# A gated attention and mixture-of-experts block on one core: short steps moved between engines, one-hot copies and the order list rearranged

## The reference, cut to what matters

```python
x = x + tanh(g_xattn) * cross_attention(layernorm(x), ctx)          # one head of 128, 512 keys
x = x + tanh(g_ffn) * ffn(layernorm(x))

def ffn(X):
    h = rmsnorm(X, norm1_w)
    q, k, v = (h @ w for w in (wq, wk, wv))                          # 16 heads of 8
    ctx = softmax(q @ k.T / sqrt(8)) @ v
    X = X + ctx @ wo
    h2 = rmsnorm(X, norm2_w)
    combine = softmax of the 2 best of 8 experts by softmax(h2 @ router_w)
    return X + swiglu(h2, shared) + sum_e combine[:, e] * swiglu(h2, expert e)
```

## Time and profile before

| | us |
|---|---|
| median of 3 executions (lowest, highest) | 221.26 (218.88, 221.61) |
| the profiled execution | 220.48 |
| its span, from the first to the last instruction | 218.6 |
| TensorE, VectorE, ScalarE, GpSimd busy | 193.9, 139.4, 106.8, 54.6 |

### The profile page before, as it was taken

One profiled execution on the slowest core, in us unless ns is written; L12 is line 12 of the kernel. 1 busy time (PEld: TensorE's weight loads), 2 busy tenths in 40 slices (PEclk: granted clock), 3 DMA queues, 4 the chain that ended last, 5 costly groups with the idle time before them and its releaser, 6 DMA issues.

```text
span 218.6 us, 4395 instructions
## 1 busy us (share of the span) xinstructions
PE 193.9 (89%) x1575; PEld 167.1 (76%) x1575; DVE 139.4 (64%) x357; ACT 106.8 (49%) x215; POOL 54.6 (25%) x88
## 2 busy tenths in 40 slices
PE   7388995997888979879898989988999999999994
PEld 5265764874866757657686859978999999999993
DVE  2604667789596766857774765889665564554653
ACT  2636374665477757958788734324222223223220
POOL 2917396122010075216841034300000000000000
PEclk9959999999999999999999999999999999999999
DMA  5941993055457935793200000000000000000000
GB/s 139 234 128 22 160 163 42 17 69 69 69 70 94 139 108 70 86 132 103 78 0 0 3 0 0 3 0 1 17 10 3 0 25 3 0 3 24 0 4 24
DMA packets 8998, 11.55 MB, mean 53 GB/s; under 512 B 976, under 2 KB 6992, under 8 KB 8752
## 3 DMA queue, kind: packets, MB, share of 16 engines
q1 hardware_dynamic: 8976, 11.27, 29.1%
HBM read 5.50 MB, written 0.52 MB: 28 GB/s over the span
## 4 chain that ended last, share of the span: by engine, by line
PE 76%; DVE 14%; ACT 4%; issue 3%; POOL 1%; DVEq 0%; POOLq 0%; ACTq 0%
PE bank L1117 14%; PE bank L1106 7%; PE bank L1105 7%; PE bank L1107 7%; PE bank L1088 7%; PE bank L1062 6%; PE bank L1073 5%; DVE mxs L849 4%; PE bank L939 4%; PE bank L954 3%; PE bank L1126 2%; PE bank L930 2%; ACT k_st L519 2%; PE bank L1010 1%; PE bank L946 1%
## 5 line engine op out<-in xcount | busy, mean ns | idle before, releaser
L849 DVE TENSOR_REDUCE mxs<-bank 128x2 f32<-128x512 f32 x64 | 41.4, 687 | 15.2 <-PE bank L1062 14.8
L637 ACT ACTIVATE ep<-bank 128x512 f32<-128x512 f32 x64 | 36.5, 605 | 14.1 <-PE bank L1073 13.6
L1105 PE MATMUL bank<-split,whi 128*128 128x256 f32 x144 | 43.2, 300 | 0.0
L1106 PE MATMUL bank<-split,whi 128*128 128x256 f32 x144 | 40.7, 283 | 0.0
L1107 PE MATMUL bank<-split,wlo 128*128 128x256 f32 x144 | 40.2, 279 | 0.0
L1117 PE MATMUL bank<-down_s,early 128*128 128x128 f32 x288 | 38.3, 276 | 2.1 <-DVE early L866 2.0
L657 ACT ACTIVATE early<-bank 128x512 f32<-128x512 f32 x28 | 16.7, 598 | 46.9 <-PE bank L1107 46.9
L1117 PEld LDWEIGHTS bank<-down_s,early 128*128 128x128 f32 x288 | 35.0, 191 | 2.6 <-DVE early L866 2.2
L869 DVE TENSOR_TENSOR early<-early,bank 128x512 f32<-128x512 f32 x28 | 19.3, 688 | 25.4 <-PE bank L1107 25.3
L1062 PE MATMUL bank<-k_st,q_st 80*128 80x256 f32 x128 | 29.7, 317 | 0.9 <-DVE mxs L849 0.5
L1105 PEld LDWEIGHTS bank<-split,whi 128*128 128x128 f32 x144 | 27.3, 190 | 0.0
(11 more groups left out here) (141 smaller groups left out, 274.2 us busy)
## 6 DMA issues: line engine op xcount, KB each, us to landing
raw<-expert_w SPq DMA_DIRECT2D x9, 256.0 KB, 8.2
k_st<-k_st SPq DMA_DIRECT2D x7, 256.0 KB, 5.8
q_st<-split SPq DMA_DIRECT2D x24, 64.0 KB
k_st<-split SPq DMA_DIRECT2D x24, 64.0 KB
down_s<-expert_w SPq DMA_DIRECT2D x9, 128.0 KB, 8.0
early<-ctx_T SPq DMA_DIRECT2D x1, 672.0 KB, 9.3
xs<-x_tiles SPq DMA_DIRECT2D x2, 256.0 KB, 4.8
out_dram<-x SPq DMA_DIRECT2D x4, 128.0 KB, 1.8
```

The source lines that it names most:

```text
L637: nc.scalar.activation(ep[:, n % NEP].rearrange("p t s -> p (t s)"), b_of(("exp", n))[:], ACT.Exp, scale=SCALE_H).then_inc(free(("exp", n) ...
L849: nc.vector.tensor_reduce(mxs[:, half % 2, :, 64 + h:65 + h], b_of(("max", n))[:].rearrange("p (t s) -> p t s", t=TB), AX_X, ALU.max).then ...
L1105: pe.matmul(bank, whi[:, fs], h2hi[:, hs], start=True, stop=False)
L1106: pe.matmul(bank, whi[:, fs], h2lo[:, hs], start=False, stop=False)
```

## The change

1. The maxima product runs over the 64 head rows alone (`NROW`), so the maxima rows of `q_st` needn't be cleared or copied: the two clearings on GpSimd, the two DMAs and step c go.
2. ScalarE writes the turned maxima once per half batch (256 columns) in place of four times (1024 columns); GpSimd copies them to the other three places (`spread_maxima`), and TensorE waits for that from the third head of a half on (`m_spread`).
3. The second layer norm's y is made by GpSimd as a step y of its own, in place of VectorE's second loop in `second_norm`.
4. x1 = x1 + gate * (y + context @ wo) is made by GpSimd in two operations (`add_context`) after h2, in place of one of VectorE's (L829) at wo; VectorE waits for it before the down product of an expert is added.
5. The two one-hot copies become steps r0 and r1 of the list; TensorE waits for them at the first product with the maxima.
6. `SEQ_STEPS`, `FIRST_STEPS` and `MIXED_STEPS` are arranged anew, with six expert items among the slots and after them in place of eight.

```diff
 SEQ_STEPS = {
-    0: [("mT0", 9, 9), ("mT1", 17, 17), ("uT0", 30, 31), ("uT1", 31, 31), ("cT", 32, 32),
-        ("wo", 36, 39), ("square", 38, 41), ("h2", 38, 42), ("h2T", 46, 46), ("router", 54, 54)],
+    0: [("mT0", 9, 9), ("mT1", 15, 16), ("uT0", 30, 31), ("uT1", 31, 31), ("cT", 32, 32),
+        ("wo", 36, 37), ("square", 36, 40), ("h2", 37, 42), ("h2T", 45, 46), ("router", 51, 52)],
     1: [("mT0", 7, 7), ("mT1", 16, 17), ("uT0", 31, 31), ("uT1", 31, 31), ("cT", 31, 31),
-        ("wo", 34, 34), ("square", 39, 39), ("h2", 39, 41), ("h2T", 44, 45), ("router", 47, 50),
-        ("route_exp1", 47, 51), ("route_top", 49, 52), ("route_exp2", 52, 56),
-        ("route_weights", 50, 58)],
-    2: [("mT0", 8, 8), ("mT1", 15, 15), ("uT0", 31, 34), ("uT1", 34, 35), ("cT", 35, 35),
-        ("wo", 40, 41), ("square", 41, 43), ("h2", 46, 49), ("h2T", 57, 60), ("router", 62, 66)],
-    3: [("mT0", 7, 9), ("mT1", 15, 15), ("uT0", 34, 36), ("uT1", 35, 42), ("cT", 41, 49),
-        ("wo", 47, 51), ("square", 51, 54), ("h2", 52, 55), ("h2T", 58, 60), ("router", 60, 62),
-        ("route_exp1", 66, 71), ("route_top", 66, 73), ("route_exp2", 75, 75),
-        ("route_weights", 90, 90)],
+        ("wo", 34, 34), ("square", 37, 37), ("h2", 41, 41), ("h2T", 44, 44), ("router", 47, 50),
+        ("route_exp1", 44, 49), ("route_top", 51, 55), ("route_exp2", 48, 54),
+        ("route_weights", 52, 57)],
+    2: [("mT0", 9, 9), ("mT1", 16, 17), ("uT0", 31, 34), ("uT1", 33, 34), ("cT", 36, 36),
+        ("wo", 39, 42), ("square", 41, 42), ("h2", 44, 44), ("h2T", 54, 56), ("router", 59, 63)],
+    3: [("mT0", 8, 9), ("mT1", 15, 15), ("uT0", 37, 39), ("uT1", 37, 44), ("cT", 39, 49),
+        ("wo", 48, 50), ("square", 49, 55), ("h2", 56, 58), ("h2T", 58, 61), ("router", 60, 68),
+        ("route_exp1", 67, 72), ("route_top", 68, 79), ("route_exp2", 68, 74),
+        ("route_weights", 85, 85)],
 }
-FIRST_STEPS = """f0 g0 xn0 f1 t0 f2 q0 s0 g1 s1 p0 xn1 z0 g2 xn2 p1 q1 o0 o1 s2 s3 f3 q2 p2 j0 p3 n0 s4 o2 h0 o3
-                 p4 k0 n1 g3 e0 xn3""".split()
-MIXED_STEPS = {0: "h1", 1: "m0 s5", 2: "k1 e1 o4", 3: "p5 q3", 4: "e2 o5 e3 w0", 6: "s6", 7: "s7 n2 h2",
-               11: "p6 m1", 12: "k2 o6", 13: "p7 o7", 14: "w1 m2", 17: "n3 h3", 26: "m3", 28: "m4 k3", 38: "c3",
-               42: "m5 m6", 43: "m7 w2", 54: "w3", 71: "m8", 74: "i0", 75: "i0", 100: "i0", 102: "i0", 106: "i0",
-               111: "i0", 132: "i0 i0"}
+FIRST_STEPS = """f0 g0 f1 g1 xn0 q0 s0 t0 s1 f2 p0 xn1 r0 j0 g2 p1 o0 q1 xn2 r1 o1 s2 s3 q2 p2 z0 f3 n0 p3 s4 g3
+                 h0 o2 y0 o3 y1 k0 n1 p4 xn3 e0 h1 s5""".split()
+MIXED_STEPS = {0: "o4", 2: "k1 q3 p5", 3: "e1 o5 e2", 4: "e3", 6: "m0", 7: "y2 s6", 8: "s7 n2 p6", 10: "w0",
+               11: "w1", 12: "h2 o6 k2", 14: "p7 o7 y3 n3", 17: "h3 m1", 24: "m2 k3", 29: "m3", 36: "m4",
+               42: "w2", 47: "m5", 50: "w3", 65: "m6 m7 m8", 75: "i0", 103: "i0 i0", 106: "i0", 117: "i0",
+               128: "i0"}
 BANKS = {"turn": (0, 1, 6), "proj": (2, 3, 7), "sum": (4, 5), "misc": (4, 5)}
...
@@ -317,11 +319,10 @@
         def copy_pads(sp, s):
-            words, maxima = k_st[:].bitcast(F32), q_st[:].bitcast(F32)
+            words = k_st[:].bitcast(F32)
             sp.dma_start(words[64:NSEL, s], words[64:NSEL, 0]).then_inc(padded[s], 16)
-            sp.dma_start(maxima[64:NSEL, s], maxima[64:NSEL, 0]).then_inc(padded[s], 16)
...
@@ -403,12 +403,33 @@
+            def layer_norm(b):
+                for i in range(b * TB, (b + 1) * TB):
+                    last = nc.gpsimd.tensor_scalar(y[:, i, :], x1[:, i, :], mv[:, 1, i, 0:1], small[:, 5, i:i + 1],
+                                                   ALU.subtract, ALU.mult)
+                last.then_inc(y_ready, 1)
+                pool.wait_ge(y_ready, b + 1)
+            def add_context(b):
+                ts = slice(b * TB, (b + 1) * TB)
+                xb, yb = (t[:, ts, :].rearrange("p t d -> p (t d)") for t in (x1, y))
+                hb = xs[:, ts, :].rearrange("p t d -> p (t d)")
+                step(nc.gpsimd.tensor_tensor(hb, yb, tg[:, 1:2].broadcast_to([P, TB * D]), ALU.mult))
+                nc.gpsimd.tensor_tensor(xb, xb, hb, ALU.add).then_inc(x_ready, 1)
+                pool.wait_ge(x_ready, b + 1)
+            def spread_maxima(b, half):
+                is_read(pool, ("mT", b, half))
+                rows = q_st[NROW:NSEL, b % NSTACK]
+                nc.gpsimd.tensor_copy(rows[:, 4 * half + 1:4 * half + 4, :],
+                                      rows[:, 4 * half:4 * half + 1, :].broadcast_to([NH, NG // 2 - 1, L])
+                                      ).then_inc(m_spread, 1)
+                pool.wait_ge(m_spread, 2 * b + half + 1)
...
@@ -512,15 +529,13 @@
-            def copy_picks(s):
-                picks = ident[64:NSEL, 64:64 + NH].rearrange("r (g p) -> r p g", p=2)
-                for p in range(2):
-                    nc.scalar.copy(k_st[64:NSEL, s, p * NG:(p + 1) * NG, :],
-                                   picks[:, p].unsqueeze(2).broadcast_to([NH, NG, L])).then_inc(picks_ready, 1)
+            def copy_picks(p):
+                picks = ident[64:64 + NH, 64:64 + NH].rearrange("r (g p) -> r p g", p=2)
+                nc.scalar.copy(k_st[64:64 + NH, 0, p * NG:(p + 1) * NG, :],
+                               picks[:, p].unsqueeze(2).broadcast_to([NH, NG, L])).then_inc(picks_ready, 1)
-            copy_picks(0)
...
@@ -595,11 +610,8 @@
-                    if b == 0 and half == 0:
-                        for i in range(1, NSTACK):
-                            act.wait_ge(padded[i], 64)
-                    rows = b_of(use)[64:NSEL, 0:L].unsqueeze(1).broadcast_to([NH, NG // 2, L])
-                    nc.scalar.mul(q_st[64:NSEL, b % NSTACK, 4 * half:4 * half + 4, :], rows, -1.0).then_inc(free(use), 1)
+                    nc.scalar.mul(q_st[NROW:NSEL, b % NSTACK, 4 * half, :], b_of(use)[NROW:NSEL, 0:L], -1.0
+                                  ).then_inc(free(use), 1)
...
@@ -729,12 +743,11 @@
             def second_norm(b):
                 dve.wait_ge(norm2_out, b + 1)
-                for k, dst, signal in ((6, xs, hs_ready), (5, y, y_ready)):
-                    for i in range(b * TB, (b + 1) * TB):
-                        last = nc.vector.scalar_tensor_tensor(out=dst[:, i, :], in0=x1[:, i, :], scalar=mv[:, 1, i, 0:1],
-                                                              in1=small[:, k, i:i + 1].broadcast_to([P, D]),
-                                                              op0=ALU.subtract, op1=ALU.mult)
-                    last.then_inc(signal, 1)
+                for i in range(b * TB, (b + 1) * TB):
+                    last = nc.vector.scalar_tensor_tensor(out=xs[:, i, :], in0=x1[:, i, :], scalar=mv[:, 1, i, 0:1],
+                                                          in1=small[:, 6, i:i + 1].broadcast_to([P, D]),
+                                                          op0=ALU.subtract, op1=ALU.mult)
+                last.then_inc(hs_ready, 1)
...
@@ -824,10 +837,6 @@
                     nc.vector.tensor_tensor(yb, b_of(("wo", b))[:, 0:TB * D], yb, ALU.add).then_inc(free(("wo", b)), 1)
-                    is_read(dve, ("wo", b))
-                    xb = x1[:, ts, :].rearrange("p t d -> p (t d)")
-                    step(nc.vector.scalar_tensor_tensor(out=xb, in0=yb, scalar=tg[:, 1:2], in1=xb,
-                                                        op0=ALU.mult, op1=ALU.add))
...
@@ -870,6 +879,7 @@
             def dense_down(n):
+                dve.wait_ge(x_ready, b + 1)
...
@@ -1045,13 +1055,9 @@
-                    if n == 0:
-                        pe.wait_ge(picks_ready, 2)
                     if h == 0:
-                            pe.wait_ge(padded[b], 64)
-                        else:
-                            pe.wait_ge(pads_ready, b // NSTACK + 1)
+                            pe.wait_ge(padded[b], 48)
@@ -1060,14 +1066,18 @@
                     may_fill(pe, ("max", n))
-                                         q_st[0:NSEL, b % NSTACK, h // 2, j * P:(j + 1) * P],
-                                         k_st[0:NSEL, b % NSTACK, k_slot(h), :], start=True, stop=True)
+                                         q_st[0:NROW, b % NSTACK, h // 2, j * P:(j + 1) * P],
+                                         k_st[0:NROW, b % NSTACK, k_slot(h), :], start=True, stop=True)
                 n = slot - LAG
+                    if n == 0:
+                        pe.wait_ge(picks_ready, 2)
                     if h % 8 == 0:
                         written(("mT", b, h // 8))
+                    if h % 8 == 2:
+                        pe.wait_ge(m_spread, 2 * b + h // 8 + 1)
```

More of the change, by code:

```diff
@@ L89, in flamingo_block @@
     NG = NH // 2
-    NSEL = 64 + NH
+    NROW = 64
+    NSEL = NROW + NH
     groups = [range(0, 2), range(2, NB)]
@@ L252, in flamingo_block @@
         zeros_ready, lower_ready = sem("zeros_ready"), sem("lower_ready")
```

(20 more changed lines are left out.)

## The result

The changed kernel takes 280.17 us (median of 4 executions, 278.48 to 283.33) against 220.44 us for the kernel before (218.88 to 221.61): a ratio of 1.269, interval 1.256 to 1.282. The profiled execution took 280.60 us, its span is 278.7 us.

What follows compares the result with a forecast made beforehand. Bound: a front with a TensorE hole, slots held by TensorE and waits for VectorE, a drain that only moves. Front -6.0 and -1.6, slots -2.0, tail +0.5, two moved steps -0.5: -9.6, so 210.9 profiled, 211.6 median; range 207.8 to 217.

Steps and rivals of the forecast that it cites:

- (f): Slots: maxima products over 64 rows in place of 80 change nothing, as weight loads of 80 and 128 rows take 190 ns.
- the 64 rows buy nothing: Rival on the slots' maxima product: the cut to 64 rows gains nothing, inside the forecast; no chance of its own given.
- The clock rival: Front: TensorE's clock falls to 0.50 as long as before, q, v and score cost 2.3 us more: 213.9; chance 0.10.
- Step (e): Slots: turned maxima of batches 2 and 3 filled later, -0.6 us; mT1 of batch 0 the other way, +0.3.
- The front to the first row maximum: Start of kernel: ScalarE's copy of x comes earlier, -6.0 us, first row maximum at about 10.3; bounds 3.7 to 6.1 earlier.
- From there to slot 0: First row maximum to slot 0: one-hot copies +0.5, shorter waits -2.1, net -1.6 us; slot 0 at about 29.1.
- The spread on GpSimd: Slots: GpSimd copies 768 columns to the other three places in 0.61 to 0.91 us, hidden from TensorE, cost 0.
- the slower rival with GpSimd in front of the spread: Slots: the maxima spread queues on GpSimd behind steps waiting for weights, 10 us and more, 221 to 228; chance 0.05.
- The tail: After the slots: six items in place of eight, the 2.00 us wait behind VectorE's routing may grow; +0.5, bounds -1.5 and +3.
- no VectorE operation over 1 us beside GpSimd: Sign that the forecast holds: no VectorE operation takes over 1 us while running beside a GpSimd operation.
- so no wait: Front: clearing the k rows moves behind norm2, to about 20 us; only early reader is ScalarE at about 27 us.
- the second rival: Front: the one-hot copies aren't hidden, cost 3.7 us and the 2.1 gain fails: +5.3, 216.9; half gives 214.3; chance 0.14.

Runs made afterwards that it cites:

- 2: Changed kernel with the maxima product over 80 rows again, plus the clearings, two DMAs and step c that it needs: 222.13 us.
- 3: Kernel before the change with its maxima product over 64 rows and nothing else: 281.67 us, ratio 1.281.
- 8: Changed kernel with 14 overwritten products of 512 columns added at slot 20, where the clock stands at half: 263.58 us.
- 4: Changed kernel with 14 overwritten products of 512 columns ahead of mT1 of batch 0, where TensorE idles at slot 15: 247.30 us (profiled) and 272.94.
- 9: Kernel of 7 with one added, overwritten product of 64 rows and 32 columns in every slot, between the two pairs: 273.27 us.
- experiment 6: The 80-row kernel (2) with 72 rows for the maxima product: 220.20 us.
- 10: Control for 9, on the kernel of 7: the same added product of 32 columns in every slot, over 80 rows: 221.01 us.
- 11: Kernel of 7 with the norm of batch 3 (n3) moved back from slot 14 to slot 17: 222.26 us.
- 7: The 80-row kernel (2) with mT1 of batch 0 two slots later, at slot 17: 219.78 us, beside 220.84 for the kernel before.
- 13: Kernel of 2 with an added product of 64 rows and 32 columns in one slot of four: 220.97 us.
- 1: Changed kernel with mT1 of batch 0 filled two slots later (17, 17 in place of 15, 16): 271.44 us, ratio to the kernel before 1.231.
- 12: Kernel of 7 with the two one-hot copies put back ahead of ScalarE's list: 222.92 us.
- 14: Changed kernel with the maxima and exponentials products both over 64 rows, plus 14 products of 512 columns at slot 20: 246.28 us.

## Why the prediction was wrong

**The step that failed** is (f) of the slots, "max products over 64 rows in place of 80: the weight load of 80 rows takes 190 ns, that of 128 rows too. Nothing." It measured +58 (2) to +61 (3): by the estimate under 8 about 15 us for changes of the row count, at 0.14 to 0.19 us each (4, 9), and the rest as the clock that the slots then could not hold. The rows that it rested on the earlier trace rows are right, and the load over 64 rows isn't longer either (185 ns at full clock). But both rows lie above 64 rows, and so does every product of the kernel before. The step carried them across a border that none of them had crossed, and it looked at how long the load takes, not at when it may start. Its rival, "the 64 rows buy nothing", had no price below nothing, though part (f) had no row at 64 to exclude a loss.

The Trainium skill has the rule: "TensorEngine Tiling (Array Packing)", section "Key Properties", says that changing the tiling mode, not just the tile, drains TensorE, and the section "Available Configurations" lists tiles of 64 rows as another mode than full rows. The trace agrees: with the clock at 1.00, starts go from 0.12 to 0.21 us and the weight load no longer runs beside the product ahead of it (4), and experiment 6 puts 72 rows on the side of 80. The sections give no price, and the products of the slots name no tile; that a plain product over 64 rows pays all the same is what 9 against 10 shows. As a rival it would have been one on the slower side; the prediction cited two others.

**The clock rival** ("falls again", 213.9, chance 0.10) had the right mechanism in the wrong place and size. It was priced for the front, as one fall that ends by itself and costs 2.3 us. The front kept 1.00 throughout in the changed kernel's profile. With 80 rows (72 in 6) the clock did fall there, at about 30 us for 6.8 us, in four of seven profiles (2, 9, 10, 11, not in 6, 7, 13), with the same wait of 1.8 us at 26.7 us in all seven. In the slots of the changed kernel the fall did not end for 16 slices. "No gap there is over 1.5 us" was no safeguard either, since in 1, 4 and 8 the clock fell with no such gap ahead (the longest 0.72 us, 0.78 us and none in the 12 us before).

**Step (e)** gave `mT1` of batch 0 +0.3. It became the wait of 3.2 us: at slot 15 it is filled right behind `p7 o7 y3 n3`, and VectorE owes it the last maximum, which waits behind the norm and its round trip to GpSimd. Worth 8.7 us in the changed kernel (280.17 to 271.44), and in the 80-row kernel about 2 (222.13 to 219.78), inside the spread of the executions.

**What held.** The front to the first row maximum: forecast -6.0 and 10.3, measured -5.5 and 10.81, and 12 confirms that the copies' place is the reason. From there to slot 0: forecast -1.6, measured -0.4 (slot 0 at 30.80, forecast 29.1); the two copies were hidden as said, but the norms and steps moved off VectorE bought next to nothing. The chain that ended last runs there through GpSimd: its new y (L408, 1.59 us at 25.75), then the powers of the next norm behind it (L387, 1.04 us at 27.41). ScalarE's row set: 374 ns for 370. The spread on GpSimd: 816 ns, between 0.61 and 0.91, and TensorE never waits for it, so the slower rival with GpSimd in front of the spread did not happen. GpSimd gained 15.0 us for 17 less two clearings. The tail: +0.5 forecast; in the 80-row kernel of 7 +2.6, with the same 2.0 us wait and a fall of the clock behind it; 10 and 11, without a fall there, have +1.6. The +5.2 of the changed kernel also hold the 6.7 us after slot 63 at half clock.

**Beside GpSimd.** The sign "no VectorE operation over 1 us beside GpSimd" did not hold, although L829 is gone. VectorE's part of the routing, in the changed kernel, where such an operation takes 190 ns elsewhere:

```profile
175.58 1.27 POOL L464 TENSOR_TENSOR wlo<-raw,whi 128x512 fp32r<-128x512 f32 x1
175.86 1.04 DVE L800 TENSOR_TENSOR rt<-rt,rs 128x32 f32<-128x32 f32 x1
```

L800 ends 0.05 us behind GpSimd's split of the weights; L808 (905 ns, usual 165) ends so behind the next split, and L724 (1149 ns at 21.74 us, usual 170) behind the clearing of the k rows, step z0, of which the prediction had said "so no wait". None of these GpSimd operations is one of the 24 new ones: the new order put old ones there. In 7 three routing operations (936, 598 and 1103 ns for 192) lie on the chain that ended last, 2.1 us longer than usual in sum; how much of its tail's +2.6 they are stays open.

**What the other parts are worth** is seen in 7: with (f) taken out, 216.6 to 217.5 us in the two executions with the higher clock, in place of the forecast 211.6. Against the sum that the forecast was made of (210.9 for a profiled execution) 7's 217.5 are 6.6 too many: 2.1 at slot 0, 2.0 in the tail, and 2.5 in the slots, which gained nothing (76.1 us from slot 0 to 63 in both) where the forecast had -2.5; the clock's fall at 60 to 64 us lies among them. One slip of the text changes nothing: half of the second rival, 214.3, lies just above the forecast's 208.5 to 214, not in it.

## What to carry to other kernels

Before the contraction length of one matmul in an interleaved stream is changed, look at its neighbours: all at 64 rows or all at 72 and more, or each change costs more than a product of 256 columns takes (0.19 against 0.12 us at full clock). Padding 64 rows to 72 or 80 with zeros was free here. Price a shape that the trace doesn't hold with a loss as its lower bound, and price a fall of TensorE's clock by whether what follows can raise it again, not by the length of the gap in front of it.

## What the runs showed of the hardware

- A change between products over 64 rows and over 72 or more costs 0.14 us (with a probe of 32 columns) to 0.19 us (between pairs of 256 columns) at full clock, and at half clock starts of 0.34 to 0.38 us in place of 0.21, 0.30 us per change. Between 64-row products it costs nothing: 0.12 us from start to start.
- At a change of the row count the next weight load starts 0.20 to 0.21 us behind the start of the product ahead, in place of 0.003 us; its own length at full clock is the same, 185 ns over 64 rows and 190 over 80.
- TensorE can be busy 69.2 of 70 us and be granted 1.2 GHz throughout (3). In a burst of 14 products of 128 rows and 512 columns it went back to 2.4 GHz (8, 14); a stream with many changes and one of 64-row products then lost it again some 30 us later without a long wait, while the 80-row slots recovered from a fall after 10.2 us (2).
- A VectorE operation of 0.17 to 0.19 us took 0.6 to 1.15 us beside a GpSimd operation and ended within 0.05 us of its end.
- The same kernel's executions differ by nearly 6 us (216.6 to 222.4) as its mean clock is 0.98 or 0.95; which gap of 1 to 2 us is followed by a fall shifts with an edit of the steps (11).
